# GpSimd raises the group norm's 64 group variances to the power minus one half, in place of ScalarE's root and VectorE's reciprocal

## The chip, the cores and the metric

The kernel runs on one core of one Trainium2 chip. The metric is the device time of one execution in microseconds (us). A core has five engines, each with its own in-order queue: TensorE (PE; its weight loads are PEld), VectorE (DVE), ScalarE (ACT), GpSimd (POOL) and SyncE (SP, which here only issues DMAs). They meet through semaphores.

## The reference, cut to what matters

Four layers run one after the other on 16 batches of 128 tokens by 256 channels: a latent cross attention with an MLP (layer 0), a grouped-query attention with a layer norm (layer 1), a recurrent block (layer 2) and a gated cross attention (layer 3). The change is in layer 2, where the output `y` of the scan is normalised over each head of 8 channels (32 heads, S = 8):

```python
y = outs.transpose(1, 0, 2, 3)                      # B, L, H, S
gm = jnp.mean(y, axis=-1, keepdims=True)
gv = jnp.mean((y - gm) ** 2, axis=-1, keepdims=True)
y = ((y - gm) * jax.lax.rsqrt(gv + EPS)).reshape(B, L, C) * gn_w + gn_b   # EPS = 1e-05
x = x + y * g @ Wo.T
```

With two batches per turn there are 2 x 32 = 64 such variances for each of the 128 tokens, which are the partitions.

## The kernel before, in words

Two batches make a turn, and there are 8 turns. The turns are pipelined in software: a phase (`start`, `first`, `second`, `steady0` to `steady4`, `closing`, `last`, `end`) holds layer 2 of one turn beside layers 0 and 1 of the next, the layer 3 of the one before, and the loads of the one after. The order of every engine's steps is written out by hand in four strings (`PE_ORDER`, `ACT_ORDER`, `DVE_ORDER`, `POOL_ORDER`); an engine issues its steps in that order and waits on semaphores, so a step that waits holds everything behind it on its engine. Layer 2 is in eight phases: `second`, the five `steady`, `closing` and `last`.

The steps around the change, in the order of their data:

- `yT` on PE (line 971) turns `y` over and subtracts each head's mean by a product with `centre`. `yT` on ACT copies the product to `yc` (line 1155) and squares it to `sq` (line 1156).
- `yn` on DVE (line 1495) sums the squares of each head into `gvar`, 64 columns. `yn` on ACT (line 1159) takes the root of `gvar/8 + 1e-5` into `gdev`; the function needs another activation table than the one loaded, so a table load stands before it. DVE takes the reciprocal into `grs` (line 1498) and multiplies `yc` by it (line 1500).
- `ynT` on PE (line 693, a transpose; in the traces its input is just `slot`) and on ACT (line 1036, with `gn_w` and `gn_b`, tensor `gn_t`), `y2` on DVE (line 1505), `o2` on PE (line 712).

Beside them, in the same few microseconds:

- `x1T` is a step of layer 0's end: PE transposes `X1`, ACT copies it out (line 1025), and POOL adds a row to `X1` into `XB1` (line 1670). `X` and `X1` share a slot, so SP loads the next turn's `x` (line 626) only when `XB1` is made (`sems["xb1"]`). PE's `xT` (line 693) waits for that load, in `second` and in the five `steady` phases; `closing` and `last` load no `x`.
- `q1` on DVE (line 1406) stands behind `yn` in DVE's order, and PE's first `scores1.0` (line 757) needs it. PE's order from there is `aT x1T q1 cT ynT scores1.0 xT o2 q0` in the steady phases, with small differences of order between them, and `yT q1 xT scores1.0 ynT q0 o2` in `second`.
- The other norms take their inverse root on POOL already (`inverse_root`, lines 1641 and 1643): an addition of the epsilon on 2 columns and a `tensor_tensor` with `ALU.pow` on 2 columns, against a tile `minus_half`. `norm3` and `norm4` follow `x1T` in POOL's order.

Of the kernel before, what the change touches and what calls it, by code (L numbers as in the profile page):

```python
# [139 lines left out]
exps0.15 turn0.14 turn0.15 sum0 d2 decay hn r2 aT g2 apply0 u0 u1 u2 u3 x1T yT yn xT ynT exps1.0 exps1.1 exps1.2 k0l  # L140
# [9 lines left out]
turn0.12 t exps0.15 turn0.13 turn0.14 exps3.0 d1 k2 turn0.15 turn3.0 exps3.1 exps3.2 exps3.3 turn3.1 d2 decay sum0 r2  # L150
turn3.2 exps3.4 g2 exps3.5 hn turn3.3 turn3.4 exps3.6 turn3.5 apply0 turn3.6 exps3.7 k3 turn3.7 u0 sum3 u1 u2 u3 aT yT
x1T yn ynT xT exps1.0 exps1.1 k0l exps1.2 exps1.3 exps1.4 xcT k0c exps1.5 exps1.6 fk exps1.7 exps1.8 fr exps1.9
exps1.10 exps1.11 x4T exps1.12 exps1.13 exps1.14 q3 exps1.15 k1 sum1 @steady2 exps0.0 exps0.1 turn0.0 exps0.2 exps0.3
turn0.1 turn0.2 turn0.3 exps0.4 exps0.5 exps0.6 exps0.7 turn0.4 turn0.5 turn0.6 exps0.8 exps0.9 turn0.7 exps0.10
turn0.8 xaT exps0.11 turn0.9 exps0.12 exps0.13 turn0.10 turn0.11 turn0.12 turn0.13 exps0.14 t turn0.14 exps0.15 d1
exps3.0 turn0.15 exps3.1 k2 d2 turn3.0 decay exps3.2 turn3.1 exps3.3 sum0 r2 turn3.2 exps3.4 exps3.5 g2 turn3.3 hn
apply0 turn3.4 turn3.5 exps3.6 exps3.7 k3 turn3.6 turn3.7 u0 u1 u2 sum3 u3 aT yT x1T yn ynT xT exps1.0 exps1.1 k0l
exps1.2 exps1.3 exps1.4 k0c xcT exps1.5 exps1.6 fk fr exps1.7 exps1.8 exps1.9 exps1.10 x4T exps1.11 exps1.12 q3
exps1.13 exps1.14 exps1.15 k1 @steady3 exps0.0 @steady2 sum1 @steady3 turn0.0 exps0.1 exps0.2 exps0.3 turn0.1 turn0.2
# [5 lines left out]
@steady4 exps0.0 exps0.1 exps0.2 exps0.3 turn0.0 turn0.1 turn0.2 turn0.3 exps0.4 exps0.5 exps0.6 exps0.7 turn0.4
turn0.5 turn0.6 turn0.7 exps0.8 exps0.9 exps0.10 turn0.8 turn0.9 exps0.11 xaT turn0.10 exps0.12 exps0.13 turn0.11
exps0.14 turn0.12 t turn0.13 turn0.14 exps0.15 d1 exps3.0 k2 turn0.15 exps3.1 turn3.0 d2 decay exps3.2 turn3.1 sum0
exps3.3 r2 turn3.2 turn3.3 exps3.4 g2 hn exps3.5 apply0 turn3.4 turn3.5 exps3.6 exps3.7 k3 u0 turn3.6 turn3.7 u1 u2 u3
sum3 yT aT x1T yn ynT xT exps1.0 exps1.1 k0l exps1.2 exps1.3 k0c xcT exps1.4 exps1.5 exps1.6 fr fk exps1.7 exps1.8 k1
# [5 lines left out]
exps1.2 exps1.3 exps1.4 xcT exps1.5 exps1.6 exps1.7 fr exps1.8 fk exps1.9 exps1.10 exps1.11 exps1.12 x4T exps1.13
exps1.14 q3 exps1.15 @last exps3.0 @closing sum1 @last turn3.0 k3 exps3.1 exps3.2 turn3.1 exps3.3 exps3.4 exps3.5
turn3.2 turn3.3 turn3.4 turn3.5 exps3.6 exps3.7 xaT turn3.6 turn3.7 t sum3 d1 k2 d2 decay r2 g2 yT yn ynT xcT fk fr
x4T q3 @end exps3.0 exps3.1 turn3.0 exps3.2 exps3.3 turn3.2 exps3.4 exps3.5 exps3.6 exps3.7 turn3.4 turn3.6 sum3
# [77 lines left out]
norm4 @steady4 scores0.0 scores0.4 scores0.8 @steady3 norm1 apply1 @steady4 sum0 scores0.12 @steady3 norm2 @steady4
scores3.0 vr0 vr1 scores3.4 scores1.0 hn vr2 gather0 vr3 gather1 vr4 gather2 vr5 gather3 vr6 gather4 vr7 gather5
gather6 gather7 x1T @closing norm3 @steady4 norm4 @closing scores0.0 scores0.4 @steady4 norm1 apply1 @closing sum0
scores0.8 @steady4 norm2 @closing scores0.12 scores3.0 vr0 vr1 hn vr2 gather0 vr3 gather1 vr4 gather2 vr5 gather3
scores3.4 vr6 gather4 vr7 gather5 gather6 gather7 norm4 x1T scores1.0 @last scores3.0 @end scores3.0 @closing norm1  # L260
# [156 lines left out]
def build(nc, x, ctx, m0, m1, m3, wl0, wl1, wl2, wl3, cols, rows, gate, out):  # L417
# [1343 lines left out]
```

## Time and profile before

| | us |
|---|---|
| device time, three runs | 1122.0, 1123.47 (median), 1125.25 |
| span of the profiled execution (first to last instruction) | 1119.7 |
| PE busy | 973.4 (87%) |
| PEld busy | 700.2 (63%) |
| DVE busy | 817.1 (73%) |
| ACT busy | 733.0 (65%) |
| POOL busy | 256.2 (23%) |

The span leaves out what lies before the first and behind the last instruction; that execution's own device time is not listed apart from the three, and the median is 3.8 us above its span. A busy share is an average over the whole span; what an engine waits for in a given place is in the timeline and in the chain of waits. Matmuls are pipelined, so a busy PE is not a PE at its peak.

### The profile page before, as it was taken

To read this page: it belongs to the slowest core of one execution; us is meant where nothing else is said; L and a number is where in the kernel's file an instruction comes from. 1 tells how busy PE (TensorE), PEld (TensorE's weight loads), DVE (VectorE), ACT (ScalarE), POOL (GpSimd) and SP (SyncE) were. 2 spreads that over 40 slices of the span, in tenths; PEclk is the share of its full clock that TensorE was granted. 3 is DMA by queue.
4 is the path that set the end of the run, shared out by engine and by line. 5 is a ranking of instruction groups with operands and counts; after the bars stand their busy time and mean duration, and the time that the engine had idled before them with its cause. 6 is when DMAs were issued, how large, how long until landed. Compare 5 with 4: busy or idle time off the path is not lost.

```text
span 1119.7 us, 23998 instructions
## 1 busy us (share of the span) xinstructions
PE 973.4 (87%) x7776; PEld 700.2 (63%) x7776; DVE 817.1 (73%) x3119; ACT 733.0 (65%) x2663; POOL 256.2 (23%) x349
## 2 busy tenths in 40 slices
PE   6779898999989899999989899989989899878365
PEld 4456566667767577756766576656766577555243
DVE  3608768977878776987878677977878687876624
ACT  2629852888568883898477882888658883882115
POOL 3210314121411332131411413031321313120300
PEclk9989999999999999999999999999999999899568
DMA  8100000000010001000010001000010000000000
GB/s 288 58 13 6 6 10 15 3 7 2 1 34 8 2 1 34 3 6 2 1 34 8 2 2 33 2 8 1 2 33 8 1 2 10 2 3 11 0 1 10
DMA packets 18667, 18.90 MB, mean 17 GB/s; under 512 B 7280, under 2 KB 16752, under 8 KB 18288
## 3 DMA queue, kind: packets, MB, share of 16 engines
q1 hardware_dynamic: 18544, 17.37, 5.0%
q8 instruction: 64, 1.05, 0.4%
q14 instruction: 59, 0.48, 0.1%
HBM read 15.27 MB, written 2.10 MB: 16 GB/s over the span
## 4 chain that ended last, share of the span: by engine, by line
PE 47%; ACT 14%; DVE 13%; issue 7%; POOL 2%; DMA 0%; DVEq 0%; POOLq 0%; ACTq 0%
PE ring L702 10%; PE ring L712 10%; ACT E L1064 9%; PE ring L768 8%; PE psS L757 4%; DVE SS L1484 3%; PE ring L933 2%; DVE S L1241 2%; PE psO L800 2%; PE ring L693 2%; PE psO L792 2%; POOL Z L1623 2%; DVE kv L1477 1%; PE psO L830 1%; PE ring L923 1%
## 5 line engine op out<-in xcount | busy, mean ns | idle before, releaser
L1064 ACT ACTIVATE E<-S,nmax 128x128 f32<-128x128 f32 (+1 forms) x1024 | 423.6, 418 | 33.1 <-PE ring L768 22.1
L1241 DVE CUSTOM_DVE_ANT_0 S<-psS,mb 128x128 f32<-128x128 f32 (+1 forms) x1024 | 261.8, 319 | 30.5 <-PE psS L757 15.1
L702 PE MATMUL ring<-slot,w_l 128*128 128x256 f32 x992 | 244.2, 393 | 18.2 <-ACT slot L1025 14.6
L768 PE MATMUL ring<-ident,E 128*128 128x128 f32 x1280 | 200.0, 286 | 45.4 <-ACT E L1064 35.6
L702 PEld LDWEIGHTS ring<-slot,w_l 128*128 128x128 f32 x992 | 185.9, 195 | 57.5 <-ACT slot L1025 17.3
L768 PEld LDWEIGHTS ring<-ident,E 128*128 128x128 f32 x1280 | 142.9, 143 | 120.3 <-ACT E L1064 79.1
L1064 ACT ACTIVATION_READ_ACCUMULATOR E<-S,nmax 128x1 f32 x1024 | 195.7, 191 | 0.0
L712 PE MATMUL ring<-w_l,slot 128*128 128x256 f32 (+1 forms) x640 | 151.6, 381 | 10.9 <-DVE slot L1505 3.5
L712 PEld LDWEIGHTS ring<-w_l,slot 128*128 128x128 f32 x640 | 114.4, 194 | 37.3 <-issue 7.5
L1257 DVE COPY ET<-ring 128x512 f32<-128x512 f32 x140 | 93.2, 685 | 31.9 <-PE ring L768 31.5
L1051 ACT ACTIVATE ET<-ring 128x512 f32<-128x512 f32 x180 | 100.3, 588 | 21.2 <-PE ring L768 20.1
L1484 DVE TENSOR_TENSOR_SCAN SS<-wP,kv 128x258 f32<-128x258 f32 x128 | 105.4, 863 | 5.7 <-POOL Z L1623 3.6
L757 PE MATMUL psS<-keys,slot 32*128 32x512 f32 (+1 forms) x768 | 95.1, 575 | 11.0 <-DVE nmax L1241 5.6
L1025 ACT ACTIVATE slot<-ring 128x512 f32<-128x512 f32 x72 | 42.6, 594 | 76.0 <-PE ring L693 57.8
L693 PE MATMUL ring<-ident,slot 128*128 128x128 f32 x384 | 63.0, 290 | 27.9 <-DVE slot L1217 7.1
L1623 POOL TENSOR_TENSOR Z<-SS,slot 128x512 f32<-128x512 f32 x64 | 79.1, 1237 | 28.0 <-DVE SS L1484 19.1
L1241 DVE DVE_READ_ACCUMULATOR2_ANT nmax<- 128x1 f32 x1024 | 85.5, 83 | 0.0
L1595 POOL TENSOR_TENSOR keys<-k0T,in 128x512 f32<-128x512 f32 x32 | 32.9, 1040 | 222.2 <-PE psS L757 215.1
L693 PEld LDWEIGHTS ring<-ident,slot 128*128 128x128 f32 x384 | 44.2, 146 | 52.2 <-issue 13.1
L792 PE MATMUL psO<-ET,V 128*32 128x128 f32 x1536 | 64.0, 283 | 4.7 <-ACT ET L1051 3.3
L1633 POOL TENSOR_TENSOR kv<-s,wP 128x4 f32<-128x4 f32 x64 | 13.2, 214 | 203.4 <-ACT slot L1025 130.5
L1441 DVE SCALAR_TENSOR_TENSOR slot<-ring,colt,slot 128x256 f32<-128x256 f32 x80 | 34.9, 478 | 32.8 <-PE ring L933 32.7
(121 smaller groups left out, 1122.7 us busy)
## 6 DMA issues: line engine op xcount, KB each, us to landing
slot<-in_ctx SPq DMA_DIRECT2D x8, 256.0 KB, 2.7
slot<-in_x SPq DMA_DIRECT2D x8, 256.0 KB, 2.7
w_l<-in_wl SPq DMA_DIRECT2D x1, 2048.0 KB, 8.4
out<-slot SPq DMA_DIRECT2D x8, 256.0 KB, 2.1
w_l<-in_wl SPq DMA_DIRECT2D x1, 1152.0 KB, 5.5
m0i<-in_m SPq DMA_DIRECT2D x8, 128.0 KB, 3.1
mb<-in_m SPq DMA_DIRECT2D x8, 128.0 KB, 2.1
w_l<-in_wl SPq DMA_DIRECT2D x3, 256.0 KB, 5.2
```

Source lines behind the costliest of these rows:

```text
L693: m = pe.transpose(b[:, c, a * P:(a + 1) * P], src[:, a, c * P:(c + 1) * P], ident[:, :])
L702: m = pe.matmul(b[:, a, :], w[:, k, m0 + a * P:m0 + (a + 1) * P], src[:, k, :], start=(k == 0), stop=(k == kt - 1))
L712: m = pe.matmul(b[:, bb, 0:n], src[:, k, bb * P:(bb + 1) * P], w[:, k, :], start=(k == 0), stop=(k == kt - 1))
L757: ins = pe.matmul(psS[m % QUAD][:, x * w:(x + 1) * w], queries, keys[rows, group % RING_K, x * w:(x + 1) * w], start=True, stop=True)
L768: m = pe.transpose(b[:, k, :], E[:, g % RING_E, k * P:(k + 1) * P], ident[:, :])
L792: m = pe.matmul(psO[32 * c:32 * c + 32, t, bb * P:(bb + 1) * P], v[:, window(8 * t + 4 * half + c, half, 16)], e, start=(half == 0 and sbl ...
L1051: act.activation(ET[:, g % 4, :, :], bank(phase, i, turned).rearrange("p a (h s) -> p (a h) s", h=2), ACT.Copy).then_inc(sems["emptied_A"], 1)
L1064: ins = act.activation(E[:, g % RING_E, h * w:(h + 1) * w], S[:, g % RING_S, h * w:(h + 1) * w], ACT.Exp, bias=nmax[:, g % 4, h:h + 1], sc ...
L1241: ins = dve.tensor_tensor_reduce(S[:, g % RING_S, h * w:(h + 1) * w], psS[g % QUAD][:, h * w:(h + 1) * w], bias[:, bb, :], -1.0, HUGE, ALU ...
L1257: dve.tensor_copy(ET[:, g % 4, :, :], bank(phase, i, turned).rearrange("p a (h s) -> p (a h) s", h=2))\
L1484: ins = dve.tensor_tensor_scan(SS[:, u % 2, a, :, :].rearrange("p b t -> p (b t)"), wP[:, ct, :, :].rearrange("p b t -> p (b t)"), kv[:, u ...
L1623: pool.tensor_tensor(Z[:, v % RING_Z, :, :].rearrange("p a (b t) -> p a b t", b=PAIR), SS[:, v % 2, :, :, 0:P], r, ALU.mult).then_inc(sems ...
```

## The change

POOL gets a step `yn`, placed in each of the eight phases right behind `gather7` and before `x1T` (in `closing` and `last` before `norm4`). It waits for `gvar`, adds 1e-5 to the 64 columns and raises them to the power minus one half with one `tensor_tensor`. ACT's step `yn` and DVE's reciprocal are gone. The division by 8 moves into ACT's squaring, as a scale of 8 ** -0.5. DVE's multiplication still follows in its step `yn`, waiting for `grs`. The orders of PE and DVE are as before; ACT's is as before without `yn`.

```diff
-        minus_half = sb("minus_half", [PAIR])
-        eps_g = sb("eps_g", [1])
+        minus_half = sb("minus_half", [64])
...
                     elif step == "yT":
                         act.wait_ge(sems["product"], product("yT"))
                         act.activation(yc, bank(phase, i, "yT"), ACT.Copy)
-                        act.activation(sq, bank(phase, i, "yT"), ACT.Square).then_inc(sems["emptied_A"], 1)
-                    elif step == "yn":
-                        act.wait_ge(sems["gvar"], turn("gvar"))
-                        act.activation(gdev[:, :], gvar[:, :], ACT.Sqrt, scale=1.0 / 8, bias=eps_g[:, :])\
-                            .then_inc(sems["gdev"], 1)
+                        act.activation(sq, bank(phase, i, "yT"), ACT.Square, scale=8 ** -0.5)\
+                            .then_inc(sems["emptied_A"], 1)
...
                             .then_inc(sems["gvar"], 1)
-                        dve.wait_ge(sems["gdev"], turn("gdev"))
-                        dve.reciprocal(grs[:, :], gdev[:, :]).then_inc(sems["rstd_g"], 1)
                         dve.wait_ge(sems["rstd_g"], turn("rstd_g"))
...
-                    pool.tensor_tensor(rs[n][:, :], veps[n][:, :], minus_half[:, :], ALU.pow)\
+                    pool.tensor_tensor(rs[n][:, :], veps[n][:, :], minus_half[:, 0:PAIR], ALU.pow)\
                         .then_inc(sems[f"rstd{n}"], 1)
...
+                    elif step == "yn":
+                        pool.wait_ge(sems["gvar"], turn("gvar"))
+                        pool.tensor_scalar(gdev[:, :], gvar[:, :], 1e-5, None, ALU.add).then_inc(sems["gdev"], 1)
+                        pool.wait_ge(sems["gdev"], turn("gdev"))
+                        pool.tensor_tensor(grs[:, :], gdev[:, :], minus_half[:, :], ALU.pow).then_inc(sems["rstd_g"], 1)
```

Of the orders, one phase of each stands for the eight (`second`, cut):

```diff
 # ACT_ORDER
-... u0 u1 u2 u3 x1T yT yn xT ynT exps1.0 ...
+... u0 u1 u2 u3 x1T yT xT ynT exps1.0 ...
 # POOL_ORDER
-... vr7 gather5 gather6 gather7 x1T norm4 ...
+... vr7 gather5 gather6 gather7 yn x1T norm4 ...
```

## Rows read from the trace of the kernel before

**Rows 1.** The chain of waits of the page, shares by engine.
```profile
PE 47%; ACT 14%; DVE 13%; issue 7%; POOL 2%; DMA 0%; DVEq 0%; POOLq 0%; ACTq 0%
```

**Rows 2.** Groups by line and shape, ACT: name, count | busy us, mean ns | idle before.
```profile
L1064 ACT ACT_TABLE_LOAD x8 | 10.3, 1283 | 0.1
L1159 ACT ACT_TABLE_LOAD x8 | 10.3, 1283 | 0.1
...
L1159 ACT ACTIVATE gdev<-gvar,eps_g 128x64 f32<-128x64 f32 x8 | 2.8, 348 | 0.1
```

**Rows 3.** The same view, DVE.
```profile
L1498 DVE RECIPROCAL grs<-gdev 128x64 f32<-128x64 f32 x8 | 4.4, 552 | 10.8 <-ACT gdev L1159 10.8
```

**Rows 4.** Lines 1643 and 1633 alone: duration ns min/median/max.
```profile
L1643 POOL TENSOR_TENSOR rs<-veps,minus_half x40: 707/707/1097, 10.5 to 1069.9; 128x2 f32<-128x2 f32 x40
...
L1633 POOL TENSOR_TENSOR kv<-s,wP x64: 200/208/390, 161.3 to 1046.0; 128x4 f32<-128x4 f32 x64
```

**Rows 5.** Timeline of the first inverse root: start, duration us, instruction, idle before, releaser.
```profile
10.15 0.22 POOL L1641 TENSOR_SCALAR veps<-mv 128x2 f32<-128x2 f32 x1 [4.60 <-DVE mv L1210]
10.45 0.71 POOL L1643 TENSOR_TENSOR rs<-veps,minus_half 128x2 f32<-128x2 f32 x1
```

**Rows 6.** Timeline of `steady0`.
```profile
313.96 1.01 DVE L1495 TENSOR_REDUCE gvar<-slot 128x64 f32<-128x512 f32 x1 [1.32 <-ACT slot L1156]
...
315.34 1.28 ACT L1159 ACT_TABLE_LOAD   x1
...
317.60 0.69 DVE L1500 TENSOR_TENSOR slot<-slot,grs 128x512 f32<-128x512 f32 x1
...
320.21 0.66 PE L693 MATMUL ring<-ident,slot 128*128 128x128 f32 x4
```

**Rows 7.** Timeline of `steady1`.
```profile
440.55 1.02 DVE L1495 TENSOR_REDUCE gvar<-slot 128x64 f32<-128x512 f32 x1 [1.77 <-ACT slot L1156]
...
443.28 0.69 DVE L1500 TENSOR_TENSOR slot<-slot,grs 128x512 f32<-128x512 f32 x1
...
446.48 0.66 PE L693 MATMUL ring<-ident,slot 128*128 128x128 f32 x4
```

**Rows 8.** Timeline of `steady2`.
```profile
566.16 1.02 DVE L1495 TENSOR_REDUCE gvar<-slot 128x64 f32<-128x512 f32 x1 [1.71 <-ACT slot L1156]
```

**Rows 9.** Chain of waits in `steady2`: start us, us, what.
```profile
566.76 1.29 POOL slot L1670
...
568.06 2.69 DMA slot<-in_x
...
570.80 0.66 PE ring L693 x4
```

**Rows 10.** Timeline of `second`.
```profile
191.15 1.02 DVE L1495 TENSOR_REDUCE gvar<-slot 128x64 f32<-128x512 f32 x1 [3.28 <-ACT slot L1156]
...
193.40 0.69 DVE L1500 TENSOR_TENSOR slot<-slot,grs 128x512 f32<-128x512 f32 x1
...
194.93 1.14 PE L757 MATMUL psS<-keys,slot 32*128 32x512 f32 x8 [1.71 <-DVE slot L1406]
```

**Rows 11.** Stretches of 4 us: PE, PEld, DVE, ACT, POOL busy, PEclk, DMA, GB/s.
```profile
60.00:64.00 4.00, 3.17 (x8) 2.55 (x9) 0.78 (x2) 0.00 (x0) 0.00 (x0) 0.50 0.00 0
64.00:68.00 4.00, 4.00 (x19) 3.50 (x18) 0.00 (x0) 1.68 (x4) 0.00 (x0) 0.92 0.00 0
...
1032.00:1036.00 4.00, 0.44 (x3) 0.03 (x1) 3.97 (x6) 0.60 (x1) 1.76 (x4) 1.00 0.00 0
1036.00:1040.00 4.00, 1.22 (x12) 1.16 (x16) 3.93 (x6) 0.00 (x0) 2.24 (x3) 0.68 0.00 0
1040.00:1044.00 4.00, 4.00 (x26) 1.91 (x24) 3.61 (x7) 0.00 (x0) 1.54 (x3) 0.50 0.00 0
```

**Rows 12.** Timeline of `last` and, the last row, of `steady0`, PE alone.
```profile
1063.96 3.78 PE L712 MATMUL ring<-w_l,slot 128*128 128x256 f32 x8 [1.84 <-DVE slot L1505]
...
309.92 1.99 PE L712 MATMUL ring<-w_l,slot 128*128 128x256 f32 x8
```

More of the change, by code:

```diff
@@ L150 @@
[L150 to L159, printed above, removed]
@@ L165 @@
[L165 to L169, printed above, removed]
@@ L175 @@
[L175 to L178, printed above, removed]
+turn3.6 turn3.7 u0 sum3 u1 u2 u3 yT aT x1T ynT xT exps1.0 exps1.1 exps1.2 k0l exps1.3 k0c xcT exps1.4 exps1.5 exps1.6
@@ new lines @@
+exps3.6 exps3.7 k3 turn3.6 turn3.7 u0 u1 u2 sum3 u3 aT yT x1T ynT xT exps1.0 exps1.1 k0l exps1.2 exps1.3 exps1.4 k0c
+xcT exps1.5 exps1.6 fk fr exps1.7 exps1.8 exps1.9 exps1.10 x4T exps1.11 exps1.12 q3 exps1.13 exps1.14 exps1.15 k1
+@steady3 exps0.0 @steady2 sum1 @steady3 turn0.0 exps0.1 exps0.2 exps0.3 turn0.1 turn0.2 turn0.3 exps0.4 exps0.5
+exps0.6 exps0.7 turn0.4 turn0.5 turn0.6 exps0.8 exps0.9 exps0.10 turn0.7 turn0.8 xaT exps0.11 turn0.9 exps0.12
+turn0.10 exps0.13 turn0.11 turn0.12 turn0.13 exps0.14 t turn0.14 exps0.15 exps3.0 turn0.15 turn3.0 exps3.1 sum0 k2 d1
@@ L252 @@
 @steady2 scores0.8 scores0.12 scores3.0 vr0 vr1 scores3.4 scores1.0 sum0 hn vr2 gather0 vr3 gather1 vr4 gather2 vr5
-gather3 vr6 gather4 vr7 gather5 gather6 gather7 x1T @steady3 norm3 @steady2 norm4 @steady3 scores0.0 scores0.4
+gather3 vr6 gather4 vr7 gather5 gather6 gather7 yn x1T @steady3 norm3 @steady2 norm4 @steady3 scores0.0 scores0.4
 @steady2 norm1 @steady3 scores0.8 @steady2 apply1 norm2 @steady3 scores0.12 scores3.0 sum0 scores3.4 scores1.0 vr0 vr1
-hn vr2 gather0 vr3 gather1 vr4 gather2 vr5 gather3 vr6 gather4 vr7 gather5 gather6 gather7 x1T @steady4 norm3 @steady3
@@ L256 @@
[L256 to L260, printed above, removed]
@@ L261 @@
-apply1 norm2 @last vr0 vr1 vr2 gather0 vr3 gather1 vr4 gather2 vr5 gather3 vr6 gather4 vr7 gather5 gather6 gather7
-norm4
+hn vr2 gather0 vr3 gather1 vr4 gather2 vr5 gather3 vr6 gather4 vr7 gather5 gather6 gather7 yn x1T @steady4 norm3
+@steady3 norm4 @steady4 scores0.0 scores0.4 scores0.8 @steady3 norm1 apply1 @steady4 sum0 scores0.12 @steady3 norm2
+@steady4 scores3.0 vr0 vr1 scores3.4 scores1.0 hn vr2 gather0 vr3 gather1 vr4 gather2 vr5 gather3 vr6 gather4 vr7
+gather5 gather6 gather7 yn x1T @closing norm3 @steady4 norm4 @closing scores0.0 scores0.4 @steady4 norm1 apply1
@@ L263 @@
+@closing sum0 scores0.8 @steady4 norm2 @closing scores0.12 scores3.0 vr0 vr1 hn vr2 gather0 vr3 gather1 vr4 gather2
+vr5 gather3 scores3.4 vr6 gather4 vr7 gather5 gather6 gather7 yn norm4 x1T scores1.0 @last scores3.0 @end scores3.0
+@closing norm1 apply1 norm2 @last vr0 vr1 vr2 gather0 vr3 gather1 vr4 gather2 vr5 gather3 vr6 gather4 vr7 gather5
+gather6 gather7 yn norm4
 """
```

54 lines of the change are left out of this document (33 added, 21 removed).

## The prediction, written before the changed kernel was run

> **What bounds the kernel now.** I read the page's chain first: no engine carries it alone, PE holds 47%, ACT and DVE 14% and 13%, POOL 2% [rows 1]. So a microsecond counts where it stands on a hand-over between engines, and the place of the change is such a hand-over. The groups of ACT then give what the removed step is made of: eight table loads of 1.28 us and eight roots of 0.35 us on line 1159. They also show what stays: eight loads on line 1064, for the first exponential behind the gelu [rows 2]. DVE's reciprocal takes 0.55 us eight times, and DVE sat idle 10.8 us ahead of it [rows 3].
>
> Then the timeline, phase by phase. In each the reader is to look at three times: the end of `gvar` (line 1495), the start of the multiplication (line 1500), and the start of PE's transpose of the next `x` (line 693). In `steady0` `gvar` ends at 314.97 and the multiplication starts at 317.60, 2.63 us later, because the table load waits behind two copies on ACT [rows 6]; `steady3` and `steady4` have the same gap. In `steady1`, `steady2` and `closing` it is 1.71 (441.57 to 443.28) [rows 7]. In `second` it is 1.23 (192.17 to 193.40) [rows 10], in `last` too. The eight gaps sum to 3 x 2.63 + 3 x 1.71 + 2 x 1.23 = 15.5 us.
>
> The second hand-over is POOL's addition of 1.27 us (1.29 in the chain) on line 1670, upon which SP loads `x`. In `steady2` it is the chain: 1.29 of POOL, 2.69 of DMA, then PE [rows 9]. In the other steady phases PE's transpose starts 0.7 to 1.0 us later than that chain would let it, since other work is ahead of it on PE.
>
> **What goes.** ACT loses 8 x (1.28 + 0.35) = 13.0 us and DVE 8 x 0.55 = 4.4 us [rows 2, 3]. That work lies inside the 15.5 us of gaps or beside other waits, so it is not added again: the gaps are replaced by what POOL needs. The scale inside the square costs nothing, the same instruction with another constant; if it did cost something it would stand on the path, just ahead of `gvar`. The larger `minus_half` is one memset at the start.
>
> **What comes.** Per turn, behind the end of `gvar`: a hop to POOL, the addition on 64 columns, a hop, the power. A two-column addition takes 0.22 us [rows 5], one of 512 columns 1.29 [rows 9], which is 0.002 us a column; so 0.34 for 64. Between addition and power lie 0.08 us [rows 5]; with as much ahead of the addition it is 0.50 us before the power begins. I call the power D, and 0.10 us more for the hop back brings DVE to its multiplication. The gap is then 0.60 + D.
>
> D is the unknown: no row has a power on more than two columns. Two columns take 0.707 us (40 times), and a plain operation on four takes 0.208 [rows 4]. So 0.50 us is the power itself.
> - From below: all of it is a start-up, and 64 columns cost only the 0.002 us each of plain arithmetic: D = 0.84.
> - From above: all 0.707 us is proportional to the columns: D = 22.6.
> - Between: 0.25 us per column on the base of a plain instruction: D = 0.208 + 64 x 0.25 = 16.2.
>
> I take 16.2. The median and the minimum of the 40 are both 0.707, so it is a fixed amount of work. A start-up of 0.5 us would be more than twice a whole plain instruction, whereas a long calculation repeated for each column explains it without anything new. It is nearest in kind to the row I have, and it is an estimate.
>
> **Where the wait lands.** In both directions the place is uncovered. DVE holds `q1` behind its `yn`, PE holds `ynT` and with it `scores1.0`, `xT`, `o2` and `q0`, ACT holds its `ynT` and all exponentials of layer 1. POOL holds `x1T`, so SP's load of `x` and of the mask behind it, and `norm3` and `norm4`. Two paths lead out of the power:
> - By `ynT`: every multiplication shifts by 0.60 + D less the old gap. Over eight phases: 8D + 4.8 - 15.5 = 8D - 10.7.
> - By the load of `x`: the power's end, 1.27 of line 1670, 0.02, 2.69 of DMA, 0.05 [rows 9], so PE's `xT` starts at the end of `gvar` + 4.53 + D. In `steady0` 319.50 + D against 320.21, so D - 0.7 [rows 6], and the same in `steady3` and `steady4`. In `steady1` 446.10 + D against 446.48, D - 0.4 [rows 7]. In `steady2` 571.71 + D [rows 8] against 570.80 [rows 9], D + 0.9. In `second` line 1670 stood ahead of `gvar` and now stands behind it: `xT` at 196.70 + D, done 0.66 later, and `scores1.0` at 197.4 + D against 194.93, D + 2.4 [rows 10].
>
> The later path decides, and it is that of `x` where an `x` is loaded; `closing` and `last` go by `ynT`, D - 1.1 and D - 0.6. Together: 8D + 2.4 - 3 x 0.7 - 0.4 + 0.9 - 1.1 - 0.6 = 8D - 0.9. With D = 16.2 that is 128.7 us.
>
> **TensorE's clock.** In a standstill of 16 us it falls. The trace shows it: at 1032 to 1040 PE was busy 0.44 and 1.22 of 4 us, and the granted clock went from 1.00 to 0.68 and then 0.50 while PE was busy again; at 60 it was 0.50 and in the next 4 us of full work 0.92 [rows 11]. 0.50 is 1.2 GHz, 1.00 is 2.4 GHz. Eight products on line 712 take 3.78 us at the low level and 1.99 at the high one [rows 12]. After each standstill come `ynT`, `scores1.0` and `o2`, which would lose 0.45, 0.9 and 1.8 us; about half of it is hidden by the wait for `x` and gone as the clock returns, so 1.6 us for seven turns (the last one runs at the low level already): 11.2 us, bounds 0 and 25.
>
> **Sum.** 128.7 + 11.2 = 139.9 us. The profiled span of 1119.7 becomes 1259.6. The median of the runs is 1123.47, 3.8 above the span for what lies around it, so the time is 1263 us. This case's own range is 1230 to 1290 (D from 13 to 17 with the bounds of the clock).
>
> **Rivals.**
> - Four columns at a time: the calculation is repeated 16 times, D = 0.208 + 16 x 0.25 = 4.2, 8 x 4.2 - 0.9 = 32.7, no price of the clock (a standstill of 4 us is like the gaps it has). 1156 us. For it: 64 columns give a loop room that 2 don't. Against: no row shows such a saving.
> - Start-up only, D = 0.84: 8 x 0.84 - 0.9 = +5.8, 1129 us. The new wait is the load of `x` behind `yn`, above all in `second` and `steady2`. For it: the chain of `steady2`. Against: the price of two columns.
> - The other side, faster: start-up only, and the later `x` is hidden, since what follows `xT` (`q0`, `k0l`) isn't needed at once. Then the path by `ynT` counts alone: 8 x 0.84 - 10.7 = -4.0, 1119.5 us. It decides where D is under 10.7 / 8 = 1.34 us. For it: the table load stands on the chain in five of the eight phases. Against: `steady2`'s chain and the price of two columns.
> - All proportional, D = 22.6: 8 x 22.6 - 0.9 + 11 = +191, 1314 us. Against: a plain instruction already has 0.2 us of base.
> - The change doesn't do what it says: the table load only moves. It can't save less than nothing here, since line 1064 keeps its eight loads either way; the Trainium skill (ScalarE: Activation LUTs, What ACT_TABLE_LOAD costs) has 1.28 us and 1.38 more of a drain for each switch. The trace has the 1.28, and ahead of the eight roots that follow it ACT is idle 0.1 us in all [rows 2]. By the page ACT would be freed of 24 us instead of 13, which changes the sum by nothing.
>
> **Chances.** Column by column 0.50; four at a time 0.27, with what lies between it and 1230; start-up with a late `x` 0.12, of which 0.08 falls within 0.3%; faster 0.05; all proportional and beyond 0.06. A difference under 0.3% (3.4 us) can't be told from none. Faster 0.05, same 0.08, slower 0.87. The range of 1128 to 1285 leaves out the faster case, the same and the proportional one, 0.19.
>
> **What would show it.** The duration of POOL's power `grs<-gdev` gives D at once: over 13 us for my case, near 4 and near 0.84 for the rivals. DVE's line 1500 waits for POOL, about 0.6 + D after `gvar`'s end, eight times. SP's load of `x` is issued D later in the steady phases, and PE's `xT` starts 4.0 us behind the end of the power. ACT has no table load on 1159 and still eight on 1064. The granted clock drops once per turn in the middle of the run. A D that isn't 16 would make it wrong by 8 us for each microsecond; a clock that stays at 1.00 by 11.

## The result, and the profile after

The changed kernel takes 1212.24 us (median; 1210.32 to 1214.45) beside 1123.47 us of the kernel before on the same chip (median; 1122.0 to 1125.25): a ratio of 1.080, interval [1.0776, 1.0820], some 90 us slower. A fourth execution of the kernel before, of 5128.6 us, stands apart from all others and is left out. The changed kernel run again gave 1.0806 [1.0784, 1.0829]. The profiled execution took 1214.45 us with a span of 1212.7 us; its mean granted clock was 0.932, before 0.966.

First the page of the changed kernel: busy time per engine, then the chain of waits by engine, then the granted clock in 40 slices.

```profile
PE 986.4 (81%) x7776; PEld 707.4 (58%) x7776; DVE 820.3 (68%) x3111; ACT 718.3 (59%) x2646; POOL 344.2 (28%) x364
...
PEclk9999997999989997999979998999989999898568
...
PE 56%; DVE 13%; ACT 12%; POOL 10%; issue 7%; DMA 1%; SPq 0%; DVEq 0%; POOLq 0%; ACTq 0%
...
L1676 POOL TENSOR_TENSOR grs<-gdev,minus_half 128x64 f32<-128x64 f32 x8 | 84.5, 10564 | 0.7
...
L1494 DVE TENSOR_TENSOR slot<-slot,grs 128x512 f32<-128x512 f32 x8 | 11.8, 1481 | 89.2 <-POOL grs L1676 89.2
```

POOL held 2% of the chain before [rows 1] and holds 10% now. The power on 64 columns takes 10.56 us, eight times 84.5 us. DVE sits idle ahead of its multiplication for 89.2 us, and all of that ended when POOL was done. The clock shows a 7 or 8 among the 9s about once in each 140 us. Next, the lines that answer to [rows 2]: ACT's table loads, by shape.

```profile
L1035 ACT ACT_TABLE_LOAD x8 | 10.3, 1283 | 0.1
L1063 ACT ACT_TABLE_LOAD x8 | 10.3, 1283 | 0.1
```

L1035 and L1063 are the old 1036 (the gelu) and 1064 (the first exponential), each with its eight loads as before. The root's eight loads [rows 2] are gone, and nothing took their place.

The timeline of `steady0`, start and duration in us, in brackets the idle time before and what ended it; it answers to [rows 6]:

```profile
328.39 1.01 DVE L1491 TENSOR_REDUCE gvar<-slot 128x64 f32<-128x512 f32 x1 [1.32 <-ACT slot L1155]
...
329.49 0.38 POOL L1674 TENSOR_SCALAR gdev<-gvar 128x64 f32<-128x64 f32 x1 [7.25 <-DVE gvar L1491]
...
329.95 10.56 POOL L1676 TENSOR_TENSOR grs<-gdev,minus_half 128x64 f32<-128x64 f32 x1
...
340.48 1.26 POOL L1663 TENSOR_TENSOR slot<-slot,rowt 128x512 f32<-128x512 f32 x1
340.55 1.74 DVE L1494 TENSOR_TENSOR slot<-slot,grs 128x512 f32<-128x512 f32 x1 [11.15 <-POOL grs L1676]
341.77 0.37 SPq L625 DMA_DIRECT2D slot<-in_x  x1
...
342.35 1.12 PE L692 MATMUL ring<-ident,slot 128*128 128x128 f32 x4 [9.57 <-DVE slot L1494]
...
343.39 2.09 PE L756 MATMUL psS<-keys,slot 32*128 32x512 f32 x8
...
345.41 0.66 PE L692 MATMUL ring<-ident,slot 128*128 128x128 f32 x4
```

From `gvar`'s end (329.40) to the multiplication (340.55) lie 11.15 us; before it was 2.63. The gap is 11.14 or 11.15 in all eight phases, 89.2 us against 15.5. PE stands still for 9.57 us. Two things come on top. DVE's multiplication takes 1.74 us where it took 0.69: it now starts in the same moment as POOL's addition and ends 0.55 us after it. And PE's transposes take 1.12 us and the scores 2.09 where they took 0.66 and 1.14. The stretches of 4 us say why (busy PE, PEld, DVE, ACT, POOL, then the granted clock):

```profile
328.00:332.00 4.00, 2.10 (x9) 1.44 (x8) 1.01 (x1) 1.75 (x4) 2.43 (x2) 1.00 0.20 66
332.00:336.00 4.00, 0.66 (x4) 0.42 (x4) 0.00 (x0) 0.00 (x0) 4.00 (x1) 0.90 0.00 0
336.00:340.00 4.00, 0.00 (x0) 0.00 (x0) 0.00 (x0) 0.00 (x0) 4.00 (x1) 0.50 0.00 0
340.00:344.00 4.00, 1.65 (x8) 1.24 (x12) 3.42 (x8) 0.50 (x2) 1.74 (x2) 0.50 0.27 68
344.00:348.00 4.00, 4.00 (x22) 2.36 (x15) 3.60 (x26) 2.39 (x4) 0.95 (x2) 0.82 0.12 36
```

PE's last transposes before the standstill ended at 332.8 and the clock was at its low level (0.50, 1.2 GHz) by 336. Work started again at 342.35. In stretches of 1 us the clock is 0.50 up to 345, 0.79 from 345 to 346 and 1.00 (2.4 GHz) from 346 on, so in this phase it was back some three microseconds after the work had resumed; the next `xT` already takes 0.66 us again.

The chain in `steady2` answers to [rows 9]. The power ends at 615.79 and `xT` starts at 619.75, 3.96 us later:

```profile
605.23 10.56 POOL L1676 TENSOR_TENSOR grs<-gdev,minus_half 128x64 f32<-128x64 f32 x1
615.76 1.26 POOL L1663 TENSOR_TENSOR slot<-slot,rowt 128x512 f32<-128x512 f32 x1
...
617.05 0.37 SPq L625 DMA_DIRECT2D slot<-in_x  x1
...
619.75 1.11 PE L692 MATMUL ring<-ident,slot 128*128 128x128 f32 x4 [1.01 <-DMA slot<-in_x]
```

Phase by phase, each period from the start of one `gvar` to the next (the last one to the end of the span). The forecast column is the prediction's own term for that phase with the measured D = 10.56 put in:

| phase | before | after | longer by | forecast with D = 10.56 |
|---|---|---|---|---|
| `second` | 122.8 | 137.8 | 15.0 | 13.0 |
| `steady0` | 126.6 | 136.7 | 10.1 | 9.9 |
| `steady1` | 125.6 | 138.6 | 13.0 | 10.2 |
| `steady2` | 127.5 | 140.0 | 12.4 | 11.5 |
| `steady3` | 128.1 | 139.4 | 11.4 | 9.9 |
| `steady4` | 125.8 | 136.7 | 10.9 | 9.9 |
| `closing` | 110.5 | 121.6 | 11.1 | 9.5 |
| `last` | 61.7 | 71.4 | 9.7 | 10.0 |
| sum | | | 93.6 | 83.6 |

One phase varies by 1 to 3 us between two profiles of the same kernel (`last` took 68.2 in a second one), so the single rows aren't to be pressed. The six periods from `second` to `steady4` together are steadier: 829.1 us in both profiles of the changed kernel, 756.4 in the kernel before.

A shorter measure says where a loss arises: the time from the start of `yT`'s product on PE (line 970; before, 971) to the start of `scores1.0` (line 756; before, 757). It is called the stretch to the scores below, and is read from the timelines. Over the seven phases that have `scores1.0` it sums to 50.8 us before and 125.0 in the changed kernel.

### The profile page after: what moved, and what is told of

Its sections match the earlier page's. It is cut to its first block, busy times and chain, and to the rows that moved or that the text cites. A ratio compares the mean times of both kernels' runs of the same rounds, so it can differ in the third digit from the quotient of the medians.

```text
span 1212.7 us, 23988 instructions
## 1 busy us (share of the span) xinstructions
PE 986.4 (81%) x7776; PEld 707.4 (58%) x7776; DVE 820.3 (68%) x3111; ACT 718.3 (59%) x2646; POOL 344.2 (28%) x364
## 3 DMA queue, kind: packets, MB, share of 16 engines
q8 instruction: 64, 1.05, 0.3%
## 4 chain that ended last, share of the span: by engine, by line
PE 56%; DVE 13%; ACT 12%; POOL 10%; issue 7%; DMA 1%; SPq 0%; DVEq 0%; POOLq 0%; ACTq 0%
PE ring L701 14%; PE ring L711 12%; ACT E L1063 8%; PE ring L767 8%; POOL grs L1676 7%; PE psS L756 6%; PE ring L692 3%; DVE S L1237 3%; PE ring L932 3%; DVE SS L1480 2%; PE psO L799 2%; PE psO L791 2%; POOL Z L1616 2%; PE psO L829 2%; PE ring L922 1%
## 5 line engine op out<-in xcount | busy, mean ns | idle before, releaser
L1063 ACT ACTIVATE E<-S,nmax 128x128 f32<-128x128 f32 (+1 forms) x1024 | 423.4, 418 | 30.6 <-PE ring L767 18.6
L1063 ACT ACTIVATION_READ_ACCUMULATOR E<-S,nmax 128x1 f32 x1024 | 195.4, 191 | 0.0
L711 PE MATMUL ring<-w_l,slot 128*128 128x256 f32 (+1 forms) x640 | 154.9, 387 | 9.2 <-DVE slot L1283 3.1
L692 PE MATMUL ring<-ident,slot 128*128 128x128 f32 x384 | 68.7, 310 | 113.4 <-DVE slot L1494 65.0
L711 PEld LDWEIGHTS ring<-w_l,slot 128*128 128x128 f32 x640 | 117.3, 198 | 37.1 <-issue 9.0
L692 PEld LDWEIGHTS ring<-ident,slot 128*128 128x128 f32 x384 | 47.9, 155 | 141.6 <-DVE slot L1494 77.2
L756 PE MATMUL psS<-keys,slot 32*128 32x512 f32 (+1 forms) x768 | 100.7, 606 | 7.5 <-DVE nmax L1237 4.8
L1676 POOL TENSOR_TENSOR grs<-gdev,minus_half 128x64 f32<-128x64 f32 x8 | 84.5, 10564 | 0.7
L1494 DVE TENSOR_TENSOR slot<-slot,grs 128x512 f32<-128x512 f32 x8 | 11.8, 1481 | 89.2 <-POOL grs L1676 89.2
```

The source lines that it names most:

```text
L692: m = pe.transpose(b[:, c, a * P:(a + 1) * P], src[:, a, c * P:(c + 1) * P], ident[:, :])
L711: m = pe.matmul(b[:, bb, 0:n], src[:, k, bb * P:(bb + 1) * P], w[:, k, :], start=(k == 0), stop=(k == kt - 1))
L756: ins = pe.matmul(psS[m % QUAD][:, x * w:(x + 1) * w], queries, keys[rows, group % RING_K, x * w:(x + 1) * w], start=True, stop=True)
L1063: ins = act.activation(E[:, g % RING_E, h * w:(h + 1) * w], S[:, g % RING_S, h * w:(h + 1) * w], ACT.Exp, bias=nmax[:, g % 4, h:h + 1], sc ...
L1676: pool.tensor_tensor(grs[:, :], gdev[:, :], minus_half[:, :], ALU.pow).then_inc(sems["rstd_g"], 1)
```

## The experiments

Each gives its ratio to the kernel before on the same chip. Their microseconds are the ratio less one, times 1123.

**The price of a power (`e1_widths`).** One run. Each phase raises another number of columns; the rest are multiplied.

```
+ n = {"second": 2, "steady": (4, 8, 16, 32, 48)[i or 0], "closing": 24, "last": 12}[phase]
+ pool.tensor_tensor(grs[:, n:], gdev[:, n:], minus_half[:, n:], ALU.mult)
+ pool.tensor_tensor(grs[:, 0:n], gdev[:, 0:n], minus_half[:, 0:n], ALU.pow)
```

> The changed kernel, but the power is taken of a different number of columns in each phase (2, 4, 8, 16, 32, 48, 24 and 12 in second, steady0 to steady4, closing and last); the other columns are only multiplied, so the group norm's values are left out there. Theory: the power costs a base and a fixed amount for each column. From the two widths at hand (2 columns 0.707 us, 64 columns 10.563 us) that is 0.389 + 0.159 n: 4 columns 1.02 us, 8 1.66, 12 2.30, 16 2.93, 24 4.20, 32 5.48, 48 8.02. Rival: it works on blocks of columns and starts at 0.25 us a column, as I had forecast from two columns, and only wide tiles are cheaper: 4 columns 1.2 us, 8 2.2, 16 4.2, then flatter, or steps between the widths. The time as a whole: 146 columns instead of 512 take 58 us off, the extra multiplications put 2 on: about 1156 us, and down to 1147 if the clock no longer falls.

Groups by shape, POOL (count, busy us, mean ns, idle before):

```profile
L1678 POOL TENSOR_TENSOR grs<-gdev,minus_half 128x48 f32<-128x48 f32 x1 | 8.0, 8037 | 0.0
L1678 POOL TENSOR_TENSOR grs<-gdev,minus_half 128x32 f32<-128x32 f32 x1 | 5.4, 5445 | 0.0
L1678 POOL TENSOR_TENSOR grs<-gdev,minus_half 128x24 f32<-128x24 f32 x1 | 4.2, 4180 | 0.0
L1678 POOL TENSOR_TENSOR grs<-gdev,minus_half 128x16 f32<-128x16 f32 x1 | 2.9, 2917 | 0.0
L1678 POOL TENSOR_TENSOR grs<-gdev,minus_half 128x12 f32<-128x12 f32 x1 | 2.3, 2285 | 0.0
L1678 POOL TENSOR_TENSOR grs<-gdev,minus_half 128x8 f32<-128x8 f32 x1 | 1.7, 1653 | 0.0
L1678 POOL TENSOR_TENSOR grs<-gdev,minus_half 128x4 f32<-128x4 f32 x1 | 1.0, 1029 | 0.0
L1678 POOL TENSOR_TENSOR grs<-gdev,minus_half 128x2 f32<-128x2 f32 x1 | 0.7, 709 | 0.0
```

From 2 to 4 columns it is 0.160 us a column, from 48 to 64 (10.56) it is 0.158: a straight line, 0.39 + 0.158 n, which meets every width within 0.07 us. There is no step at four or sixteen columns, so the price is paid anew for each column, and the rival of four at a time falls. The forecast's 0.25 a column had taken the plain instruction's 0.21 off the 0.71 of two columns; the line takes off 0.39. The whole took 1155.47 us.

**Half the columns (`e3_half`).** The power on 32 columns, the other 32 multiplied.

```
- pool.tensor_tensor(grs[:, :], gdev[:, :], minus_half[:, :], ALU.pow)
+ pool.tensor_tensor(grs[:, 32:], gdev[:, 32:], minus_half[:, 32:], ALU.mult)
+ pool.tensor_tensor(grs[:, 0:32], gdev[:, 0:32], minus_half[:, 0:32], ALU.pow)
```

> The changed kernel with the power on 32 of the 64 columns in all eight phases, the other 32 multiplied only (their values are left out). The power takes 5.5 instead of 10.6 us and the multiplication adds about 0.35, so each turn waits 4.7 us less, 38 us in all. Theory one, every microsecond of the wait counts and nothing else: 1214 - 38 = 1176 us, ratio 1.046. Theory two, part of the 90 us is TensorE's clock, which falls some 5 to 7 us into the standstill and would now hardly fall: another 5 to 10 us less, 1168 us, ratio 1.039. Rival: the wait is partly hidden, so halving it takes away more than half of the loss or less than 30 us.

1.0457 [1.0437, 1.0476], +51.3 us; the gap is 6.24 us eight times. From here to the changed kernel the gap grows by 4.91 us, eight times 39.3; the time grows by 38.8 (90.1, the mean of both batches, less 51.3). So in this reach each microsecond of POOL's power counts in full, in each phase. The clock falls here too, in the same place of `steady0` (columns as above):

```profile
328.00:332.00 4.00, 0.91 (x4) 0.72 (x4) 2.71 (x4) 0.00 (x0) 2.49 (x2) 0.82 0.12 8
332.00:336.00 4.00, 4.00 (x16) 2.18 (x16) 3.56 (x21) 1.69 (x4) 0.95 (x2) 0.50 0.33 94
```

**No power at all (`e2_plain`).** Everything as in the changed kernel, but POOL multiplies the 64 columns instead of raising them.

```
- pool.tensor_tensor(grs[:, :], gdev[:, :], minus_half[:, :], ALU.pow)
+ pool.tensor_tensor(grs[:, :], gdev[:, :], minus_half[:, :], ALU.mult)
```

> The changed kernel with a plain multiplication in place of the power (the inverse root is left out, so the group norm's values are not those of the reference). It stands for a power that costs its start-up at most: D about 0.35 us. By the rule of my sum, the later of the two paths, it is 8 x 0.35 - 0.9 = +1.9 us and some 3 us for DVE's multiplication beside POOL's addition: ratio 1.002 to 1.004. By the path of ynT alone it is 8 x 0.35 - 10.7 = -7.9 us: ratio 0.993. If the first holds, the change would not have been faster even with a cheap power; if the second, the forecast's rival on the faster side had the right mechanism and only the price of the power decided.

1.0036 [1.0023, 1.0049], +4.0 us. POOL's and DVE's instructions alone (duration min/median/max in ns):

```profile
L1676 POOL TENSOR_TENSOR grs<-gdev,minus_half x8: 317/318/319, 191.6 to 1066.7; 128x64 f32<-128x64 f32 x8
...
L1494 DVE TENSOR_TENSOR slot<-slot,grs x8: 691/1738/1745, 191.9 to 1067.0; 128x512 f32<-128x512 f32 x8
```

The gap is 0.90 us, 8.3 us less over eight phases than the kernel before has, and the time is longer. With D = 0.32 the path by `ynT` alone gives 8 x 0.32 - 10.7 = -8.1 us; the path by `x` gives 8 x 0.32 - 0.9 = +1.7. The faster side is refuted: even a power that costs next to nothing would not have made this kernel faster. The timelines show where the loss is. In `second` and in `steady2` PE's `xT` waits for the load of `x`, 5.35 and 1.67 us:

```profile
195.95 1.11 PE L692 MATMUL ring<-ident,slot 128*128 128x128 f32 x4 [5.35 <-DMA slot<-in_x]
...
575.64 0.66 PE L692 MATMUL ring<-ident,slot 128*128 128x128 f32 x4 [1.67 <-DMA slot<-in_x]
```

There the stretch to the scores is 2.3 and 1.4 us longer than before (9.27 against 7.01, 8.85 against 7.45). In the other five phases it is between 0.2 longer and 0.8 shorter.

**The addition ahead of the power (`e5_behind_x1T`).** POOL's order is turned back, so `x1T`, and with it the load of `x`, does not wait for the power.

```
- ... gather7 yn x1T ...
+ ... gather7 x1T yn ...
```

> The changed kernel with POOL's step yn behind x1T instead of ahead of it in the six phases that load an x. The load of x then starts 11 us earlier than in the changed kernel, and POOL's addition no longer lies beside DVE's multiplication (0.69 us again). The power starts later where x1T comes late: by 1.7 us in steady0, 3 and 4, 1.0 in steady1, 0.8 in steady2, nothing in second. Theory A: second wins 3.5 us, since its transpose of x waited for the load, steady2 wins 1, steady1 nothing, steady0, 3 and 4 lose 0.6 each: 2 to 3 us faster than the changed kernel, ratio 1.077. Theory B, x decides in all six phases: each steady phase wins 1 us or more besides, 1206 us or less, ratio 1.073. In both the loss against the kernel before stays at 80 us or more, since it is the power's.

1.0758 [1.0734, 1.0781], +85.1, 5.4 us less than the changed kernel of the same batch (1.0806). DVE's multiplication is back at its 0.69:

```profile
L1494 DVE TENSOR_TENSOR slot<-slot,grs x8: 692/693/693, 203.1 to 1147.9; 128x512 f32<-128x512 f32 x8
```

In exchange the power starts later where the addition stood in its way: the gaps are 11.1 to 12.8, 95.6 us in all and so 6.4 more than in the changed kernel. That is as much as the six multiplications save (6 x 1.05 = 6.3). So of 90 us, 85 stay when the load of `x` is taken out of the matter. The path by `ynT` costs nearly as much as that of `x`; they run side by side.

**The addition behind the multiplication (`e6_apart`).** To keep DVE and POOL from running together, the addition waits until the multiplication is done.

```
  if phase in ("second", "steady"):
+     pool.wait_ge(sems["yn"], turn("yn"))
```

> The changed kernel, but in second and the steady phases POOL's addition on X1 (upon which x is loaded) waits until DVE has done the multiplication by the inverse root. In the changed kernel the two start together and DVE's takes 1.74 us instead of 0.69. Theory A, from the changed kernel's trace: with the overlap gone DVE's multiplication takes 0.69 again, and since in steady0, 1, 3 and 4 the path by ynT comes last, these four win about 1.05 us each; steady2 and second go by the load of x, which comes 0.7 to 0.8 later: 1.5 lost. In all 2 to 3 us faster than the changed kernel, ratio 1.077 to 1.078. Theory B, that of my prediction: the load of x decides in all six phases, so each loses 0.8 us: 5 us slower, ratio 1.084. Theory C: the 1.74 us has nothing to do with POOL's addition and stays.

1.0870 [1.0842, 1.0898], +97.7: 7 us slower than the changed kernel. The multiplication took 0.69, but the load of `x` was issued 13.3 us after `gvar`'s end instead of 12.4, and `xT` waited for it:

```profile
341.70 0.69 DVE L1494 TENSOR_TENSOR slot<-slot,grs 128x512 f32<-128x512 f32 x1 [11.15 <-POOL grs L1678]
...
342.56 1.27 POOL L1665 TENSOR_TENSOR slot<-slot,rowt 128x512 f32<-128x512 f32 x1 [0.90 <-DVE slot L1494]
...
343.86 0.37 SPq L625 DMA_DIRECT2D slot<-in_x  x1
...
346.43 0.66 PE L692 MATMUL ring<-ident,slot 128*128 128x128 f32 x4 [0.85 <-DMA slot<-in_x]
```

Of the theories in the expectation, B (some 5 us slower) comes nearest. A microsecond saved on DVE is worth less than 0.9 us lost on the way to `x`. That the two instructions are slow side by side is a fact; removing it so does not pay.

**The changed kernel once more (`after_again`)**, to compare the two above with it on one chip.

> The changed kernel as it is, for comparison on the same chip with the two beside it: ratio 1.080 to the kernel before, about 1213 us.

1.0806 [1.0784, 1.0829], span 1211.3.

**The gap of the kernel before, cut (`e7_early_root`).** In the kernel before, a root of one column stands ahead of ACT's wait for `yT`, so the table is loaded before it is wanted. Nothing else changes.

```
+ act.activation(early[:, :], eps_g[:, :], ACT.Sqrt)
```

> The kernel before with one more root on ScalarE, of one column of a constant, ahead of its wait for yT in the eight phases. The table of the root is then loaded while ScalarE is idle (10 to 24 us there), and the root of the 64 columns follows gvar without a load. Nothing is left out. Theory: in steady0, 3 and 4 the gap from the end of gvar to the multiplication goes from 2.63 to about 1.3 us, in steady1, steady2 and closing from 1.71 to 1.0, in second and last from 1.23 to 1.0; where the load of x doesn't decide, that is 3 x 1.3 + 2 x 0.7 = 5 us at most: ratio 0.9955 to 0.998. Rival: the load of x and other waits hide it, within 0.1% of the kernel before. The other rival: the added root's load delays the step ahead of yT, slower by up to 2 us.

The eight gaps shrink from 15.5 to 8.6 us, and the time does not: 1.0021 [0.9996, 1.0046]. In `steady0` the multiplication starts 1.21 us after `gvar` instead of 2.63, and then PE waits for another thing:

```profile
316.36 1.10 DVE L1502 TENSOR_TENSOR slot<-slot,grs 128x512 f32<-128x512 f32 x1
...
317.97 1.09 PE L694 MATMUL ring<-ident,slot 128*128 128x128 f32 x8 [0.42 <-DMA slot<-in_ctx]
...
320.07 0.66 PE L694 MATMUL ring<-ident,slot 128*128 128x128 f32 x4
```

The transposes wait for the load of `ctx`, and `xT` starts at 320.07 where it was 320.21 [rows 6]. The same wait for `ctx` stands in `steady3` and `steady4` (0.17 and 0.24 us), so there a part of the shorter gap is covered. DVE's multiplication takes 1.10 us in these three phases, in which POOL's addition began 0.7 us before it (at 315.65 in `steady0`); it ends 0.54 to 0.55 us after the addition again.

But the edit also costs something, and the null result is a balance. In `steady1` and `steady2` ACT's order has `aT` ahead of `yT`, so the early table load doesn't fall into ACT's idle time. It stands between the copy for `aT` and the copies for `yT`. First the kernel before in `steady1`, then `e7_early_root`:

```profile
439.44 0.59 ACT L1155 ACTIVATE slot<-ring 128x512 f32<-128x512 f32 x1
...
441.06 1.99 PE L702 MATMUL ring<-slot,w_l 128*128 128x256 f32 x8 [1.24 <-ACT slot L1025]
...
439.20 1.28 ACT L1155 ACT_TABLE_LOAD   x1
...
440.61 0.58 ACT L1157 ACTIVATE slot<-ring 128x512 f32<-128x512 f32 x1
...
442.21 1.99 PE L703 MATMUL ring<-slot,w_l 128*128 128x256 f32 x8 [2.76 <-ACT slot L1026]
```

PE waits 2.76 us there instead of 1.24, and `gvar` starts 3.74 us after `yT`'s product instead of 2.23. The stretch to the scores is 1.2 and 1.7 us longer in these two phases and 0.2 to 0.7 shorter in the other five (2.3 in all). So this run doesn't show that the old gaps were free. It shows that the edit gave back about as much as it took, which is the last rival of its expectation.

**`x` loaded early: `e12_own_slot`, `e10_both`, `e11_after_own_slot`.** The input `x` gets a tile of its own and is loaded right behind `ctx`, so it no longer waits for POOL's addition. `e12_own_slot` is the kernel before with that, `e10_both` has the early root as well, `e11_after_own_slot` is the changed kernel with it.

```
- X, XB2, X1 = tm(1), tm(1), tm(1)
+ X = sb("x_in_slot", [512])[:, :].rearrange("p (b c) -> p b c", b=PAIR)
+ XB2, X1 = tm(1), tm(1)
...
- sp.wait_ge(sems["xb1"], turn("xb1"))
+ sp.wait_ge(sems["xb2"], turn("xb2"))
```

> The kernel before with the incoming x in a tile of its own alone. Theory: the load of x ends 0.7 to 1.0 us ahead of its use in most phases already and is late by 0.5 us in steady2 only, so with the gaps as they are 0 to 1 us is won: ratio 0.999 to 1.000. Rival: x and ctx now load side by side, ctx lands later, and the transposes of ctx, which already waited 0.2 to 0.3 us in three phases, cost 1 to 3 us: ratio 1.001 to 1.003.

1.0012 [0.9994, 1.0029]: nothing.

> The kernel before with the table of the root loaded early and the incoming x in a tile of its own. The early table alone took 6.9 us out of the eight gaps and nothing out of the time. Theory: it gave nothing because the load of x came last in those phases; with both off the path 4 to 6 us come back, ratio 0.995 to 0.997, faster than both kernels. Rival: something else than x follows the group norm (DVE's order, the load of ctx), and the ratio stays within 0.998 to 1.002.

1.0030 [1.0010, 1.0049]: the gaps are 8.6 us and `x` is early, and still nothing is gained; it is 1 to 5 us slower. The trace has the same table load ahead of `yT` in `steady1` and `steady2`. PE waits 2.75 us there, the clock falls, and the eight products behind the wait take 2.80 and 3.78 us instead of 1.99. The stretch to the scores is 2.4 and 3.0 us longer in these two phases. So it was not the late `x` that ate the gain of `e7_early_root`.

> The changed kernel with the incoming x in a tile of its own, loaded right behind the load of ctx once the additions on the x before are done, and no longer behind POOL's addition on X1. Nothing is left out. It takes the load of x off the power without moving POOL's steps. Theory: second wins 3.6 us (its transpose of x waited for the load) and steady2 1, the others nothing, since in them ynT and scores come last: 1209 to 1210 us, ratio 1.076, as in the run with x1T ahead of yn. DVE's multiplication still takes 1.74 us beside POOL's addition. Rival: x was hidden in the changed kernel and nothing moves, ratio 1.080.

1.0766 [1.0744, 1.0789], +86.0: some 4 us less than the changed kernel. With `e5_behind_x1T` this is the second way of taking `x` out, and they give 4 and 5 us. That is what the late `x` costs in the changed kernel. It costs it in two phases: the stretch to the scores falls from 19.60 to 17.07 us in `second` and from 19.37 to 18.08 in `steady2`, and in the five others it doesn't move.

**The clock: `e4_busy_pe` and `e9_busy_pe_20`.** While POOL raises, PE multiplies weights into a bank that `ynT` (in `second`, `xT`) overwrites, so it does not stand still: 40 products (52 in `second`) in the first, 20 (26) in the second.

```
+ for n in range(20 if phase != "second" else 26):
+     pe.matmul(b[:, n % 2, :], W0["w1"][:, 0, 0:P], W0["w1"][:, 0, 0:T], start=True, stop=True)
```

> The changed kernel, with 40 products of 128x256 (52 in second) on TensorE into the bank that it will fill anyway, ahead of its wait for the normalised tile (in second ahead of its wait for x). Nothing is left out; the products are overwritten. At 0.24 us each they fill 9.6 us (12.5) of the standstills of 9.6 to 15.7 us. Theory: the granted clock stays at 1.00 through the standstills and the products behind them run at the high level (scores 1.14 instead of 2.09 us, ynT 0.66 instead of 1.12), which gives back 5 to 12 us: 1202 to 1209 us, ratio 1.069 to 1.075. Rival: the clock's fall is hidden behind DVE, ACT and the load of x, and the time stays within 3 us of the changed kernel's 1214 (ratio 1.080).

1.1263 [1.1244, 1.1282]. It tells nothing of the clock: each product is two records of 0.22 us, 40 of them 18 us, and the standstill is 10. PE was busy past the power's end in each phase.

```profile
338.72 13.55 PE L691 MATMUL ring<-w_l 128*128 128x256 f32 x62
```

> The changed kernel with 20 products of 128x256 (26 in second) on TensorE ahead of its wait, where the run before had 40: a product of fp32 is two passes and takes 0.45 us, so 20 fill 9.0 us of standstills of 9.6 us and more, and none should be left when the tile is ready. Nothing is left out. Theory: the granted clock stays at 1.00, scores takes 1.14 instead of 2.09 us and ynT 0.66 instead of 1.12 behind the standstill, and where the load of x allows it 1 to 1.5 us a turn come back: 7 to 10 us, 1204 to 1207 us, ratio 1.071 to 1.074. Rival: the clock's fall is hidden behind the load of x and DVE; within 3 us of the changed kernel, ratio 1.078 to 1.083.

1.0862 [1.0835, 1.0889], +96.7, more than the changed kernel. But in `second` and the steady phases the clock stayed at 1.00 while the products ran; in `steady0` (columns as above):

```profile
332.00:336.00 4.00, 4.00 (x20) 3.54 (x19) 0.00 (x0) 0.00 (x0) 4.00 (x1) 1.00 0.00 0
336.00:340.00 4.00, 4.00 (x20) 3.51 (x20) 0.47 (x1) 0.00 (x0) 4.00 (x2) 1.00 0.00 0
340.00:344.00 4.00, 2.79 (x19) 1.26 (x17) 3.97 (x9) 1.02 (x2) 1.55 (x3) 1.00 0.31 98
```

In `steady0`, `steady3` and `steady4` the scores take 1.14 us again. In `second` and `steady2` the products had ended and PE stood waiting for `x` (3.87 and 1.59 us), the clock fell, and the scores took 2.09 as in the changed kernel; in `steady1` it fell behind the scores. The six periods from `second` to `steady4` sum to 824.6 us; in the changed kernel to 829.1, so it is 4.6 less. The three in which the clock stayed up make up 3.3 of it (4.4 against the second profile of the changed kernel), 1.1 to 1.5 us each. In `closing` the products had to wait for a bank and ran after the standstill instead of in it:

```profile
1017.44 0.60 PE L698 MATMUL ring<-ident,slot 128*128 128x128 f32 x4
1028.39 11.06 PE L691 MATMUL ring<-w_l 128*128 128x256 f32 x40 [10.35 <-DVE V L1301]
1039.29 0.60 PE L698 MATMUL ring<-ident,slot 128*128 128x128 f32 x4
```

That period is 130.8 us long instead of 121.6, 9.2 us lost, and this hides the gain in the total. The total missed its expectation; the reading of 4.6 us stands on the periods of one profile, and since the clock still fell in half of the six phases it is a lower bound.

## Why the prediction was right, and which term was wrong

The direction held, and so did the mechanism in the main: a power paid anew for each column, on an uncovered hand-over. The time was forecast at 1263 us and was 1212. The range that held, 1128 to 1285, is wide because it joins the main case with two rivals. The main case's own range of 1230 to 1290 was missed (its bounds, D from 13 to 17, give 1227 to 1284). The measured time falls into the 0.27 of "four at a time, with what lies between it and 1230", and D was neither "over 13" nor "near 4". By its steps:

- **The power, D = 16.2 us: wrong, it is 10.56.** That is the term that was mis-sized. The chosen account (paid anew for each column) was right; the split of the 0.707 us into base and columns was not. Subtracting a plain instruction's 0.21 us left 0.25 us a column; `e1_widths` shows 0.158 on a base of 0.39. Eight times 5.64 us, it is 45 of the 51 us by which the forecast was too long.
- **Hops of 0.60 us: right.** The gap is 11.15 with a power of 10.56, so 0.59.
- **`xT` 4.0 us behind the power's end: right** in `steady2` (3.96) and `second` (4.1). In the other four it was 4.9 to 5.2, since the scores at the low clock stood ahead of it on PE.
- **The sum 8D - 0.9: nearly right.** With D = 10.56 it is 83.6 us. With D = 0.32 it gives 1.7 where 4.0 was measured [1.0023, 1.0049].
- **The later path decides, and it is that of `x` in all six phases: right in two of them.** In `second` and `steady2` PE waits for `x`, in `e2_plain` (2.3 and 1.4 us longer there) as in the changed kernel, and `e11_after_own_slot` takes 2.5 and 1.3 us out of just these two. In the other four the path by `ynT` comes last. The prediction had it shorter than it is, for the reason in the next item.
- **Not foreseen: DVE's multiplication at 1.74 us beside POOL's addition, six times.** The prediction counted each at its price alone. It adds 6 x 1.05 = 6.3 us to the path by `ynT`, which was 8D - 10.7 = 73.8, so 80.1 with the measured D. The two ways of taking `x` out agree with it: `e11_after_own_slot` has these 6.3 us, `e5_behind_x1T` has 6.4 us of longer gaps in their place, and they measured 86.0 and 85.1 us with the price of the clock in them. So the prediction's credit of 15.5 us for the old gaps isn't contradicted.
- **The clock, 11.2 us: probably too large.** It falls once per turn as forecast. `e9_busy_pe_20` saves 4.6 us in six phases, a lower bound; the 1.1 to 1.5 us of a phase in which the clock stayed up would make 8 to 10 us for seven turns, an estimate from those three phases. A second reading is argued and not shown: between `e2_plain` (gap 0.90, +4.0 us) and `e3_half` (gap 6.24, +51.3) the time grows by 47.3 where eight times 5.34 is 42.7, 4.6 more, while from `e3_half` on, where the clock already falls, it grows by the gap alone. That difference has some 3 us of uncertainty (the intervals are 0.1 to 0.2% wide to either side). So the price lies between some 4 and 10 us, and which it is stays open.
- **What goes from ACT, 13.0 us: right**, and counted inside the gaps, not beside them. The eight loads of the root are gone, those of the gelu and of the exponential stand. The rival that the load only moves falls. What was freed lay in front of waits: ahead of its next copy in `steady0`, ACT now sits idle for 13.75 us.

Added up from separate sources: 89.2 - 15.5 = 73.7 us for the longer gaps and 6.3 for the multiplications, both from the traces; 4 for the late `x` (`e11_after_own_slot`); 4.6 at least for the clock (`e9_busy_pe_20`). That is 88.6 or a little more, measured 90.1. Of the prediction, 83.6 + 4.6 = 88.2.

The rivals: four at a time and start-up only are refuted by the widths; the faster one by `e2_plain`; all proportional (D = 22.6) by the 10.56. No version that was run beats the kernel before.

## What to carry to other kernels

A single duration of a short instruction can't be split into a base and a price per column; what the row of two columns bounds is a wide range, and here a second width would have settled the forecast. A power on POOL is paid for each column (0.158 us here), so it fits the two columns of a layer norm and not 64 on a path with a hand-over at both ends. And a gap that has shrunk is not yet time won. `e7_early_root` took 6.9 us of gaps away and the time stayed, partly since another wait stood behind the gap (`ctx`), and partly since the moved table load delayed other copies in two phases. A null result of an edit that moves work has to be read phase by phase before it is called "covered".

## What the runs showed of the hardware beyond that

- DVE's two-input multiplication of 128x512 is held up by POOL's two-input addition: 0.69 us alone, 1.74 when both start together, 1.10 when POOL started 0.7 us before. It ends 0.54 to 0.55 us after the addition in both cases. The addition itself keeps its 1.26. The Trainium skill (GPSIMD Engine Reference, section 1, Specifications) says that the two engines share their way to SBUF and that GpSimd then contends with VectorE instructions of two SBUF inputs; the trace agrees, and adds that here all the loss falls on VectorE.
- During the power DVE had nothing to do in any of the eight phases (it waits from `gvar`'s end to its multiplication), so whether a power holds DVE up in the same way is not shown.
- The granted clock fell to 0.50 in a standstill of 9.6 us, and around the shorter one of `e3_half` too. In `steady0` it was back at 1.00 some 3 us after the work had resumed, in the other phases up to `closing` after 4 to 8 us. It had fallen 2 to 5 us after PE stopped, not the 5 to 7 of the expectation of `e3_half`. In `steady0` the slow scores and transposes took 1.4 us more (2.09 against 1.14, 1.12 against 0.66), and the phases in which `e9_busy_pe_20` kept the clock up became 1.1 to 1.5 us shorter.
